# Attention's first score and query units: from two PSUM banks to six

## The chip, the cores and the metric

The kernel runs on one core of a Trainium2 chip, as one program. The metric is the device time in microseconds (us). The shown runs of the kernel before took 2261.34, 2261.57 and 2262.76 us; the median is 2261.57 us.

## The reference

The input `x` has 8 sequences of 2048 rows of 256 numbers, in fp32. The reference, cut to what matters:

```python
xn = layernorm(x)
qkv = xn @ W_qkv; q, k, v = split(qkv, 3)
scores = (q @ k.T) / sqrt(256), future positions masked
attn = softmax(scores) @ v                       # causal, one head, per sequence
ids = argmax(xn @ gate_w); s = sigmoid(max(xn @ gate_w))
shared = silu(xn @ sg) * (xn @ su) @ sd
routed = expert ids of (xn * s): silu(. @ rg) * (. @ ru) @ rd    # 32 experts, top 1
out = x + attn + shared + routed
```

## The kernel before

The program has three stages on all engines, one behind the other: tokens (layer norm, shared expert, values), experts (routed expert tiles), attention. Every fp32 product is made of three matmuls of rounded parts, high by high, low by high and high by low (`split_matmuls`, lines 87 to 89), so each operand is split into a high part (a copy on ScalarE, ACT in the profile) and a low part (a subtraction on VectorE, DVE, or on GpSimd, POOL).

Attention works on 32 groups of 512 query rows (4 in each sequence), and on tiles of a group by 128 keys. Tile t is (sequence, group in it, key block); there are 320. The first groups have 4, 8, 12 and 16 tiles: tiles 0 to 3 are group 0, 4 to 11 group 1, 12 to 23 group 2, and group 3 begins with tile 24. The last four tiles of a group lie on the diagonal: they are 512, 384, 256 and 128 columns wide. The queries are `x` times a product of the weights, so a score is a query unit times the normalized input.

**Units.** What TensorE (PE) writes for a score tile or for one half of a group's queries is a unit, and takes one PSUM bank. A full unit is six matmuls of 512 columns. Units are numbered in the order in which PE makes them: tiles 0 to 8 are units 0 to 8, then come query half (2, 0) as unit 9, tiles 9 and 10, query half (2, 1) as unit 12, tile 11 as unit 13, tiles 12 to 20 as units 14 to 22, and query half (3, 0) as unit 23. Here (g, c) is half c of group g. Tiles 0 and 1 are computed at the end of the expert stage (`first_scores`).

**Steps.** `Plan` writes out the order. The engines walk the same steps, each in its own queue. At a step, PE makes the query halves and the score tile of that step, broadcasts a group's maxima (line 1735), transposes a group's running maxima (`turn`, line 1728), and, from step 25 on (LAG), weighs the values with tile step - 25 (`weigh`, lines 1749 to 1753). ACT copies a unit out of PSUM (line 1672, or line 1663 for the high part of a query half) and takes the exponentials (lines 1679 and 1680). DVE takes the low part of a query half (line 1578), masks the diagonal (line 1592), keeps the running maximum (lines 1595 to 1613), reduces the transposed maxima (lines 1617 and 1621) and adds them to the scores (`lower`, line 1628). The four tiles of group 0 are lowered early, at steps 7 to 10, and exponentiated at steps 8 to 11; all others wait for their turn after step 23. The transposes of group 0 stand at step 5 and those of group 1 at step 13; the broadcasts stand two steps later. Score tile 12 is the first that needs the low part of query half (2, 1).

**Banks.** PSUM has 8 banks here: two for units (`psS`), two for maxima (`psX`), four for the weighted sums (`psO`). The four of `psO` are used by the expert stage under other names (`e_psT`, `e_psH`, two `e_psG`); in attention they lie unused until `weigh` of tile 0 at step 25. Unit n goes to bank n modulo 2, and `free_bank(n)` makes PE wait until unit n - 2 has been read: for a query half by DVE's subtraction, for a score tile by ACT's copy, DVE's mask and DVE's maximum.

**The other queues at this place.** SyncE (SP) ends the expert stage, then issues two loads of rows and ten loads of values (512 KB each), after GpSimd has set three small constants (lines 1556 to 1558), which the first broadcast waits for too. GpSimd then gathers routed rows, subtracts the low parts of the probabilities (line 1551) and adds up rows.

Of the kernel before, what the change touches and what calls it, by code (L numbers as in the profile page):

```python
# [19 lines left out]
F32 = mybir.dt.float32  # L20
# [1319 lines left out]
class Plan:  # L1340
# [3 lines left out]
    BANKS = 2  # L1344
# [3 lines left out]
    def __init__(self, B, NB, GB):  # L1348
        J = NB // GB
        self.J, self.GB = J, GB  # L1350
        self.tiles = [(b, G, j) for b in range(B) for G in range(GB) for j in range(J * (G + 1))]
        self.at = {tile: t for t, tile in enumerate(self.tiles)}
        self.T = len(self.tiles)
        self.first = [self.at[b, G, 0] for b in range(B) for G in range(GB)]
        self.last = [self.at[b, G, J * (G + 1) - 1] for b in range(B) for G in range(GB)]
        self.NGR = B * GB
        q_step = {}
        for g in range(2, self.NGR):
            for u in range(2):
                q_step.setdefault(max(0, self.first[g] - 3 + 2 * u), []).append((g, u))  # L1360
        self.q_step = q_step
        self.q_unit, self.s_unit = {}, []
        self.split, self.tops, self.reads, self.diags, self.acts = [], [], [], [], []
        self.turn_step = {}
        for g in range(self.NGR):
            self.turn_step.setdefault(self.first[g] + self.LAG - 8 if g >= 2 else self.last[g] + 2, []).append(g)
        self.lead = self.LAG - J - 8
        self.base_step = {}
        per = J * (GB + 1) * GB // 2
        for r in range(B * NB):  # L1370
            i = r % NB
            t = max(0, (r // NB) * per + (i * per // NB if r // NB < B - 1 else 7 * i // 4) - 8)
            self.base_step.setdefault(t + self.LAG - self.LOW, []).append(r)
        n = 0
        for t in range(self.T):
            for g, c in q_step.get(t, ()):
                self.q_unit[g, c] = n
                self.split.append(n)
                self.acts.append((self.acts[-1] if n else 0) + 1)
                n += 1  # L1380
            self.s_unit.append(n)
            _, G, j = self.tiles[t]
            diagonal, rest = self.diagonal(t), self.cut(t) < J - 1
            tops = self.tops[-1] if t else 0
            self.reads.append(tops + (rest if diagonal else j > 0))
            self.tops.append(self.reads[t] + diagonal)
            self.diags.append((self.diags[-1] if t else 0) + diagonal)
            self.acts.append((self.acts[-1] if n else 0) + (rest or not diagonal))
            n += 1
        self.splits = {n: k + 1 for k, n in enumerate(self.split)}  # L1390

    def tile_at(self, step, ahead):

# [33 lines left out]
def attention_stage(nc, ctx, block, sh_g, d_rows, xth_g, xtl_g, vh_g, vl_g, out_g, keep, ahead, D, B, N, ET):  # L1427
    C, NB, GB = D // P, N // P, N // GT
    J = GT // P
# [4 lines left out]
    SR = LAG - 1  # L1434
    NGR, R = plan.NGR, B * NB
    with ExitStack() as st:
# [3 lines left out]
        def ps(name, shape):  # L1440
            return st.enter_context(nc.psum_tensor("t_" + name, shape, F32))
# [23 lines left out]
        psS, psX = ahead.psS, ahead.psX  # L1465
        assert BANKS == psS.shape[1]
        psO = ps("psO", [P, J, 512])
        x_in = ahead.x_in
        v_in = [sem(f"v_in{k}") for k in range(VR)]
        r_in = [sem(f"r_in{k}") for k in range(2)]  # L1470
# [101 lines left out]
        def _(dve):  # L1572
            v = nc.vector

            def q_low(g, c):
                n = plan.q_unit[g, c]
                wait(dve, u_act, plan.acts[n])
                v.tensor_tensor(q_lo[:, g % QR, c], psS[:, n % BANKS], q_hi[:, g % QR, c].bitcast(F32),  # L1578
                                ALU.subtract).then_inc(split_ok, 1)

            def highest(t):
                n, g, c0 = plan.s_unit[t], plan.group(t), plan.cut(t) * P
                _, G, j = plan.tiles[t]
                m, s = top[:, g % TR], psS[:, n % BANKS]
                if j == 0 and G > 0:
                    return
                if plan.diagonal(t):
                    own, c1 = slice(c0, c0 + P), c0 + P
                    wait(dve, u_mm, n + 1)
                    wait(dve, u_act, plan.acts[n])  # L1590
                    wait(dve, lo_ok, t - SR + 1)
                    v.tensor_tensor(score[:, t % SR, own], s[:, own], keep.mask[:], ALU.add).then_inc(diag_ok, 1)
                    if j == 0:
                        wait(dve, top_mm, g - TR + 1)
                        v.tensor_copy(m[:, c1:], s[:, c1:]).then_inc(top_ok, 1)
                    else:
                        wait(dve, top_ok, plan.tops[t - 1])
                        if c1 < GT:
                            v.tensor_tensor(m[:, c1:], m[:, c1:], s[:, c1:], ALU.max).then_inc(top_ok, 1)
                    wait(dve, diag_ok, plan.diags[t])  # L1600
                    if j == 0:
                        v.tensor_copy(m[:, own], score[:, t % SR, own]).then_inc(top_ok, 1)
                    else:
                        v.tensor_tensor(m[:, own], m[:, own], score[:, t % SR, own], ALU.max).then_inc(top_ok, 1)
                    return
                wait(dve, u_act, plan.acts[n])
                if j < 2:
                    wait(dve, top_mm, g - TR + 1)
                if j == 1:
                    v.tensor_tensor(m[:], score[:, (t - 1) % SR], s[:], ALU.max).then_inc(top_ok, 1)  # L1610
                else:
                    wait(dve, top_ok, plan.tops[t - 1])
                    v.tensor_tensor(m[:], m[:], s[:], ALU.max).then_inc(top_ok, 1)  # L1613
# [40 lines left out]
        @block.scalar  # L1654
        def _(act):
            s = nc.scalar

            def q_high(g, c):
                n = plan.q_unit[g, c]
                wait(act, u_mm, n + 1)  # L1660
                if g >= QR:
                    wait(act, u_mm, plan.s_unit[plan.last[g - QR]] + 1)
                s.copy(q_hi[:, g % QR, c], psS[:, n % BANKS]).then_inc(u_act, 1)

            def keep_score(t):
                n = plan.s_unit[t]
                c0 = (plan.cut(t) + plan.diagonal(t)) * P
                if c0 == GT:
                    return
                wait(act, lo_ok, t - SR + 1)  # L1670
                wait(act, u_mm, n + 1)
                s.copy(score[:, t % SR, c0:], psS[:, n % BANKS, c0:]).then_inc(u_act, 1)  # L1672

            def exps(t):
                c0 = plan.cut(t) * P
                p = score[:, t % SR, c0:]
                wait(act, sub_ok, t + 1)
                wait(act, pv_mm, t - HR + 1)
                s.activation(p_hi[:, t % HR, c0:], p, ACT.Exp)  # L1679
                s.activation(p, p, ACT.Exp).then_inc(exp_ok, 1)  # L1680

            for step in range(T + LAG + 2):
                for g, c in plan.q_step.get(step, ()):
                    q_high(g, c)
                if step < T:
                    keep_score(step)
                t = plan.tile_at(step, plan.EXP)
                if t is not None:
                    exps(t)

        @block.tensor
        def _(pe):
            def free_bank(n):
                m = n - BANKS
                if m in plan.splits:
                    wait(pe, split_ok, plan.splits[m])
                elif m >= 0:
                    t = plan.s_unit.index(m)
                    wait(pe, u_act, plan.acts[m])
                    wait(pe, diag_ok, plan.diags[t])  # L1700
                    wait(pe, top_ok, plan.reads[t])

            def queries(g, c):
                n, k = plan.q_unit[g, c], g % XR
                if c == 0:
                    wait(pe, x_in[k], 32 * ((g + XR - GB) // XR))
                free_bank(n)
                project(nc, psS[:, n % BANKS], keep, x_hi[:, k], x_lo[:, k], c).then_inc(u_mm, 1)

            def scores(t):  # L1710
                n, g, c0 = plan.s_unit[t], plan.group(t), plan.cut(t) * P
# [4 lines left out]
                    wait(pe, split_ok, plan.splits[plan.q_unit[g, C - 1]])  # L1716
                free_bank(n)
                for d in range(C):
                    mm = split_matmuls(nc, psS[:, n % BANKS, c0:], x_hi[:, k, d, cols], x_lo[:, k, d, cols],
                                       q_hi[:, q, d, c0:], q_lo[:, q, d, c0:], d == 0, d == C - 1)  # L1720
                mm.then_inc(u_mm, 1)

# [15 lines left out]
            def weigh(t):  # L1738
# [5 lines left out]
                for a in range(plan.cut(t), J):  # L1744
                    cols = slice(a * P, (a + 1) * P)
                    last = j == J * G + a
                    if j == 0:
                        wait(pe, o_ok, (g - 1) * J + a + 1)
                    nc.tensor.matmul(psO[:, a, 0:W], p_hi[:, kp, cols], v_hi[:, kv, j % J], start=j == 0, stop=False,  # L1749
# [126 lines left out]
```

## Time and profile before

| what | value |
|---|---|
| median of the runs shown | 2261.57 us |
| time of the profiled execution | 2262.84 us |
| its span, first to last instruction | 2260.9 us |
| mean granted clock of TensorE | 0.998 |
| PE busy | 2228.1 us (99%) |
| DVE, ACT, POOL busy | 1637.5, 1159.9, 1073.5 us |

The span is what the profile's clock runs over: a position in the profile is us from its start. 1.94 us of the profiled execution lie outside. Attention's part begins near 1354.7 us. A matmul's row gives its start and its duration; matmuls are pipelined, so that the spacing of starts and not the duration says how fast they go. Idle time stands in brackets behind a row, with the instruction that ended it. [...]

### The profile page before, as it was taken

To read this page: it belongs to the slowest core of one execution; us is meant where nothing else is said; L and a number is where in the kernel's file an instruction comes from. 1 tells how busy PE (TensorE), PEld (TensorE's weight loads), DVE (VectorE), ACT (ScalarE), POOL (GpSimd) and SP (SyncE) were. 2 spreads that over 40 slices of the span, in tenths; PEclk is the share of its full clock that TensorE was granted. 3 is DMA by queue.
4 is the path that set the end of the run, shared out by engine and by line. 5 is a ranking of instruction groups with operands and counts; after the bars stand their busy time and mean duration, and the time that the engine had idled before them with its cause. 6 is when DMAs were issued, how large, how long until landed. Compare 5 with 4: busy or idle time off the path is not lost.

```text
span 2260.9 us, 46624 instructions
## 1 busy us (share of the span) xinstructions
PE 2228.1 (99%) x15254; PEld 2056.2 (91%) x15254; DVE 1637.5 (72%) x3543; ACT 1159.9 (51%) x2190; POOL 1073.5 (47%) x1016
## 2 busy tenths in 40 slices
PE   8999999999999999999999998999999999999998
PEld 7888888888888999999999997999999999999998
DVE  7777777777768987877878775666666667676755
ACT  4334334334344665665656654555555555555555
POOL 3333333333324434434434433666666666666677
PEclk9999999999999999999999999999999999999999
DMA  7665665665546877777787784243434343434341
GB/s 249 217 212 187 217 212 194 210 214 197 186 147 219 278 256 256 240 266 255 248 259 256 251 250 146 94 134 113 157 111 164 111 152 120 149 126 145 121 123 45
DMA packets 299531, 423.16 MB, mean 187 GB/s; under 512 B 35777, under 2 KB 216002, under 8 KB 299330
## 3 DMA queue, kind: packets, MB, share of 16 engines
q1 hardware_dynamic: 281986, 384.48, 50.6%
q0 software_dynamic: 17344, 36.27, 6.1%
q8 instruction: 93, 1.52, 0.3%
q14 instruction: 108, 0.88, 0.1%
HBM read 281.92 MB, written 138.74 MB: 186 GB/s over the span
## 4 chain that ended last, share of the span: by engine, by line
PE 94%; DVE 2%; POOL 1%; issue 1%; DMA 1%; ACT 1%; SPq 0%; POOLq 0%; ACTq 0%; DVEq 0%
PE ahead_psS L87 10%; PE ahead_psS L88 10%; PE ahead_psS L89 10%; PE ahead_psX L87 7%; PE ahead_psX L89 7%; PE ahead_psX L88 7%; PE t_psO L1749 6%; PE t_psO L1751 5%; PE t_psO L1753 5%; PE e_psG L87 3%; PE e_psG L89 3%; PE e_psG L88 3%; PE a_psD L89 3%; PE a_psD L87 3%; PE a_psD L88 3%; PE a_psT L87 1%
## 5 line engine op out<-in xcount | busy, mean ns | idle before, releaser
L1551 POOL TENSOR_TENSOR t_p_lo<-t_score,t_p_hi 128x512 fp32r<-128x512 f32 (+1 forms) x320 | 360.0, 1131 | 200.2 <-ACT t_score L1680 116.1
L1672 ACT COPY t_score<-ahead_psS 128x512 f32<-128x512 f32 (+3 forms) x288 | 148.4, 516 | 334.0 <-PE ahead_psS L89 288.7
L1749 PE MATMUL t_psO<-t_v_hi,t_p_hi 128*128 128x258 f32 x1088 | 313.4, 288 | 3.8 <-DVE ahead_dout L1637 2.5
L1751 PE MATMUL t_psO<-t_v_hi,t_p_lo 128*128 128x258 f32 x1088 | 307.6, 283 | 0.0
L1753 PE MATMUL t_psO<-t_v_lo,t_p_hi 128*128 128x256 f32 x1088 | 306.6, 282 | 0.0
L1067 POOL DMA_INDIRECT ahead_rows<-xs_rows,ahead_slot x144 | 175.8, 1221 | 206.3 <-PE e_psT L1247 162.3
L354 POOL DMA_INDIRECT token_of<-a_token_i,a_slot_i x128 | 140.6, 1099 | 244.5 <-DVE a_slot_i L465 206.8
L87 PE MATMUL ahead_psS<-ahead_q_hi,ahead_x_hi 128*128 128x512 f32 (+3 forms) x640 | 234.7, 367 | 7.2 <-DVE ahead_q_lo L1578 3.3
L88 PE MATMUL ahead_psS<-ahead_q_hi,ahead_x_lo 128*128 128x512 f32 (+3 forms) x640 | 233.9, 365 | 0.0
L89 PE MATMUL ahead_psS<-ahead_q_lo,ahead_x_hi 128*128 128x512 f32 (+3 forms) x640 | 233.2, 364 | 0.0
L1749 PEld LDWEIGHTS t_psO<-t_v_hi,t_p_hi 128*128 128x128 f32 x1088 | 206.0, 189 | 13.0 <-DVE ahead_dout L1637 3.0
L1751 PEld LDWEIGHTS t_psO<-t_v_hi,t_p_lo 128*128 128x128 f32 x1088 | 206.3, 190 | 8.2
L1753 PEld LDWEIGHTS t_psO<-t_v_lo,t_p_hi 128*128 128x128 f32 x1088 | 206.4, 190 | 0.0
L1613 DVE TENSOR_TENSOR t_top<-t_top,ahead_psS 128x512 f32<-128x512 f32 x144 | 98.9, 687 | 135.3 <-ACT t_score L1672 134.7
L1628 DVE TENSOR_TENSOR t_score<-ahead_psX,t_score 128x512 f32<-128x512 f32 (+1 forms) x320 | 190.2, 602 | 1.3 <-PE ahead_psX L1735 1.3
L1679 ACT ACTIVATE t_p_hi<-t_score 128x512 fp32r<-128x512 f32 (+1 forms) x320 | 182.6, 571 | 13.4 <-PE t_psO L1753 10.4
L1680 ACT ACTIVATE t_score<-t_score 128x512 f32<-128x512 f32 (+1 forms) x320 | 178.3, 557 | 0.0
L1535 POOL DMA_INDIRECT ahead_dout<-routed_rows,keep_position x128 | 123.0, 961 | 111.3 <-POOL ahead_raw L1543 59.3
L87 PE MATMUL ahead_psX<-e_whi,e_h_hi 128*128 128x256 f32 x576 | 161.9, 281 | 0.2 <-DVE e_h_lo L1109 0.2
L707 ACT ACTIVATE a_silu<-ahead_psX 128x512 f32<-128x512 f32 x128 | 76.5, 597 | 166.1 <-PE ahead_psX L89 161.3
L88 PE MATMUL ahead_psX<-e_whi,e_h_lo 128*128 128x256 f32 x576 | 161.6, 281 | 0.0
L89 PE MATMUL ahead_psX<-e_wlo,e_h_hi 128*128 128x256 f32 x576 | 161.6, 281 | 0.0
(266 smaller groups left out, 7180.5 us busy)
## 6 DMA issues: line engine op xcount, KB each, us to landing
ahead_raw<-in_L_ffn_routed_gate_w SPq DMA_DIRECT2D x42, 512.0 KB
ahead_raw<-in_L_ffn_routed_up_w SPq DMA_DIRECT2D x42, 512.0 KB
ahead_raw<-in_L_ffn_routed_down_w SPq DMA_DIRECT2D x41, 512.0 KB
e_raw<-in_L_ffn_routed_gate_w SPq DMA_DIRECT2D x41, 512.0 KB
e_raw<-in_L_ffn_routed_up_w SPq DMA_DIRECT2D x41, 512.0 KB
e_raw<-in_L_ffn_routed_down_w SPq DMA_DIRECT2D x41, 512.0 KB
a_xt<-in_L_attn_x SPq DMA_DIRECT2D x32, 512.0 KB, 6.0
v_high<-a_v_hi SPq DMA_DIRECT2D x32, 512.0 KB, 3.9
```

The lines of the kernel that those rows point to most:

```text
L87: nc.tensor.matmul(out, hi, rhi, start=first, stop=False, skip_group_check=True)
L88: nc.tensor.matmul(out, lo, rhi, start=False, stop=False, skip_group_check=True)
L89: return nc.tensor.matmul(out, hi, rlo, start=False, stop=last, skip_group_check=True)
L1067: g.indirect_dma_start(out=xg[:, k, h], out_offset=None, in_=xs, in_offset=bass.IndirectOffsetOnAxis(slot[:, s, h:h + 1], 0)).then_inc(x_i ...
L1551: g_.tensor_tensor(p_lo[:, t % LR, c0:], score[:, t % SR, c0:], p_hi[:, t % HR, c0:].bitcast(F32), ALU.subtract).then_inc(lo_ok, 1)
L1628: v.tensor_tensor(s, psX[:, g % 2, c0:], s, ALU.add).then_inc(sub_ok, 1)
L1672: s.copy(score[:, t % SR, c0:], psS[:, n % BANKS, c0:]).then_inc(u_act, 1)
L1679: s.activation(p_hi[:, t % HR, c0:], p, ACT.Exp)
L1680: s.activation(p, p, ACT.Exp).then_inc(exp_ok, 1)
L1749: nc.tensor.matmul(psO[:, a, 0:W], p_hi[:, kp, cols], v_hi[:, kv, j % J], start=j == 0, stop=False, skip_group_check=True)
L1751: nc.tensor.matmul(psO[:, a, 0:W], p_lo[:, t % LR, cols], v_hi[:, kv, j % J], start=False, stop=False, skip_group_check=True)
L1753: mm = nc.tensor.matmul(psO[:, a, 0:D], p_hi[:, kp, cols], v_lo[:, kv, j % J, 0:D], start=False, stop=last, skip_group_check=True)
```

## The change

`Plan` gives every unit a bank and remembers which unit had that bank before it. Units 0 and 1 keep banks 0 and 1. The units up to 20, which are those made before tile 19, go round six banks: 2, 3, 4, 5, 0, 1, and again; banks 2 to 5 are the four of `psO`. From unit 21 (tile 19) on it is bank n modulo 2 as before. `free_bank(n)` waits for the reads of the unit that had the bank before, and not at all where there was none. `weigh` of tile 0 waits, before its first matmul into each bank of `psO`, for the reads of the last unit there (units 20, 15, 16 and 17). All readers take the unit's bank from the same list. Nothing is computed otherwise, and no engine's order changes.

```diff
+        wide = self.s_unit[self.LAG - 6]
+        self.bank, self.former, latest = [], [], {}
+        for m in range(n):
+            if m < self.BANKS:
+                bank = m
+            elif m < wide:
+                bank = (m - self.BANKS) % (self.BANKS + J)
+                bank = bank + self.BANKS if bank < J else bank - J
+            else:
+                bank = m % self.BANKS
+            self.bank.append(bank)
+            self.former.append(latest.get(bank, -1))
+            latest[bank] = m
+        self.latest = {b: max(m for m in range(wide) if self.bank[m] == b) for b in range(self.BANKS, self.BANKS + J)}
...
+        unit = [psS[:, k] if k < BANKS else psO[:, k - BANKS] for k in plan.bank]
...
-            def free_bank(n):
-                m = n - BANKS
+            def read_out(m):
                 if m in plan.splits:
                     wait(pe, split_ok, plan.splits[m])
                 elif m >= 0:
...
+            def free_bank(n):
+                read_out(plan.former[n])
+
...
                     last = j == J * G + a
+                    if t == 0:
+                        read_out(plan.latest[BANKS + a])
                     if j == 0:
                         wait(pe, o_ok, (g - 1) * J + a + 1)
```

In `q_low`, `highest`, `q_high`, `keep_score`, `queries` and `scores`, `psS[:, n % BANKS]` becomes `unit[n]`.

## Rows read from the trace of the kernel before

**Rows 1.** The page: busy time of PE, and the chain by engine.
```profile
PE 2228.1 (99%) x15254; PEld 2056.2 (91%) x15254; DVE 1637.5 (72%) x3543; ACT 1159.9 (51%) x2190; POOL 1073.5 (47%) x1016
...
PE 94%; DVE 2%; POOL 1%; issue 1%; DMA 1%; ACT 1%; SPq 0%; POOLq 0%; ACTq 0%; DVEq 0%
```

**Rows 2.** Waits of PE, whole span: total us, times, longest.
```profile
PE ahead_psS L87 <- DVE ahead_q_lo L1578: 3.3, 4, 1.4
...
PE ahead_psS L87 <- DVE t_top L1602: 1.9, 1, 1.9
PE ahead_psS L87 <- DVE t_top L1610: 1.6, 2, 0.8
...
PE ahead_psS L87 <- DVE t_top L1599: 0.4, 1, 0.4
```

**Rows 3.** Waits of PE from 1402 us to the end.
```profile
PE t_psO L1749 <- DVE ahead_dout L1637: 2.5, 2, 2.3
PE t_psO L1749 <- POOL t_p_lo L1551: 1.2, 1, 1.2
```

**Rows 4.** Windows: busy us of PE, PEld, DVE, ACT, POOL; clock, DMA share, GB/s.
```profile
1358.00:1360.00 2.00, 1.58 (x7) 1.24 (x7) 1.18 (x5) 0.00 (x0) 0.00 (x0) 0.77 0.02 4
1360.00:1362.00 2.00, 2.00 (x7) 1.52 (x6) 0.00 (x0) 0.58 (x1) 0.32 (x3) 0.50 0.19 66
1362.00:1364.00 2.00, 2.00 (x11) 1.68 (x10) 0.23 (x1) 0.59 (x1) 0.97 (x1) 0.88 0.62 176
...
1372.00:1378.00 6.00, 3.79 (x20) 3.05 (x21) 4.87 (x12) 3.62 (x11) 3.93 (x5) 1.00 1.09 352
```

**Rows 5.** Timeline of PE: start, duration, line, operation, idle before and releaser.
```profile
1354.58 0.28 PE L89 MATMUL ahead_psX<-e_wlo,e_h_hi 128*128 128x256 f32 x1
...
1375.82 0.29 PE L87 MATMUL ahead_psS<-ahead_q_hi,ahead_x_hi 128*128 128x128 f32 x1
...
1376.39 0.28 PE L89 MATMUL ahead_psS<-ahead_q_lo,ahead_x_hi 128*128 128x128 f32 x1
...
1377.47 0.47 PE L87 MATMUL ahead_psS<-ahead_q_hi,ahead_x_hi 128*128 128x512 f32 x1 [0.81 <-DVE ahead_q_lo L1578]
...
1380.33 0.60 PE L1728 MATMUL ahead_psX<-keep_ident,t_top 128*128 128x128 f32 x4
1380.68 0.48 PE L87 MATMUL ahead_psS<-ahead_q_hi,ahead_x_hi 128*128 128x512 f32 x1
...
1389.37 0.47 PE L87 MATMUL ahead_psS<-ahead_q_hi,ahead_x_hi 128*128 128x512 f32 x1
...
1392.48 0.47 PE L87 MATMUL ahead_psS<-ahead_x_hi,keep_a_hi 128*128 128x512 f32 x1
...
1402.62 0.28 PE L1749 MATMUL t_psO<-t_v_hi,t_p_hi 128*128 128x258 f32 x1
```

**Rows 6.** Timeline of DVE, 1363 to 1376 us.
```profile
1363.77 0.69 DVE L1617 TENSOR_REDUCE t_negmax<-ahead_psX 128x4 f32<-128x512 f32 x1 [4.38 <-PE ahead_psX L1728]
...
1372.66 0.69 DVE L1578 TENSOR_TENSOR ahead_q_lo<-ahead_psS,ahead_q_hi 128x512 fp32r<-128x512 f32 x1 [1.91 <-ACT ahead_q_hi L1663]
1373.27 0.41 DVE L1628 TENSOR_TENSOR t_score<-ahead_psX,t_score 128x256 f32<-128x256 f32 x1
...
1374.12 0.85 DVE L1604 TENSOR_TENSOR t_top<-t_top,t_score 128x128 f32<-128x128 f32 x1
...
1375.58 0.69 DVE L1604 TENSOR_TENSOR t_top<-t_top,t_score 128x128 f32<-128x128 f32 x1
```

**Rows 7.** Timeline of ACT: copy of tile 8 and what follows it.
```profile
1369.21 0.48 ACT L1672 COPY t_score<-ahead_psS 128x384 f32<-128x384 f32 x1 [1.03 <-PE ahead_psS L89]
1369.71 1.28 ACT L1679 ACT_TABLE_LOAD   x1
```

**Rows 8.** Timeline of POOL: last of three constants; last gather before weighing.
```profile
1361.46 0.13 POOL L1558 MEMSET t_v_hi<- 128x20 f32 x1
...
1389.30 0.96 POOL L1535 DMA_INDIRECT ahead_dout<-routed_rows,keep_position  x1 [0.83 <-POOL ahead_raw L1543]
```

More of the change, by code:

```diff
@@ L1577, in q_low @@
                 wait(dve, u_act, plan.acts[n])
-                v.tensor_tensor(q_lo[:, g % QR, c], psS[:, n % BANKS], q_hi[:, g % QR, c].bitcast(F32),
+                v.tensor_tensor(q_lo[:, g % QR, c], unit[n], q_hi[:, g % QR, c].bitcast(F32),
                                 ALU.subtract).then_inc(split_ok, 1)
@@ L1583, in highest @@
                 _, G, j = plan.tiles[t]
-                m, s = top[:, g % TR], psS[:, n % BANKS]
+                m, s = top[:, g % TR], unit[n]
                 if j == 0 and G > 0:
@@ L1662, in q_high @@
                     wait(act, u_mm, plan.s_unit[plan.last[g - QR]] + 1)
-                s.copy(q_hi[:, g % QR, c], psS[:, n % BANKS]).then_inc(u_act, 1)
+                s.copy(q_hi[:, g % QR, c], unit[n]).then_inc(u_act, 1)
             def keep_score(t):
@@ L1671, in keep_score @@
                 wait(act, u_mm, n + 1)
-                s.copy(score[:, t % SR, c0:], psS[:, n % BANKS, c0:]).then_inc(u_act, 1)
+                s.copy(score[:, t % SR, c0:], unit[n][:, c0:]).then_inc(u_act, 1)
             def exps(t):
@@ L1707, in queries @@
                 free_bank(n)
-                project(nc, psS[:, n % BANKS], keep, x_hi[:, k], x_lo[:, k], c).then_inc(u_mm, 1)
+                project(nc, unit[n], keep, x_hi[:, k], x_lo[:, k], c).then_inc(u_mm, 1)
             def scores(t):
@@ L1718, in scores @@
                 for d in range(C):
-                    mm = split_matmuls(nc, psS[:, n % BANKS, c0:], x_hi[:, k, d, cols], x_lo[:, k, d, cols],
+                    mm = split_matmuls(nc, unit[n][:, c0:], x_hi[:, k, d, cols], x_lo[:, k, d, cols],
                                        q_hi[:, q, d, c0:], q_lo[:, q, d, c0:], d == 0, d == C - 1)
```

## The prediction

> **What bounds the kernel now.** I read the page first. PE is busy 2228.1 of 2260.9 us and holds 94% of the chain that ended last [rows 1]: a microsecond that PE saves is kept, unless another engine then becomes late. Next come the waits of PE over the whole span. Waits of score and query units for DVE's reads amount to 3.3 + 1.9 + 1.6 + 0.4 = 7.2 us [rows 2], all of them between 1356 and 1400 us, where attention begins. The reader is to see there that the releasers are the last readers of a unit two places earlier: with two banks, PE makes a unit and the one after it, and then stands until DVE has done with the first. After 1402 us PE waits 3.7 us in three places, all near the end, for DVE's outputs and POOL's low parts [rows 3]; no bank wait is left there, since weighing a tile lies between two units. So the question is how far PE's clock of events moves up between 1354.7 us, where the last expert matmul ends its turn [rows 5], and 1392.48 us, where query half (3, 0) begins [rows 5]. From there both kernels have two banks and the same order.
>
> The listed waits are not the whole loss. In the windows of 2 us from 1358 to 1364 us the granted clock reads 0.77, 0.50 and 0.88 [rows 4]: time lost is 2 x 0.23 + 2 x 0.50 + 2 x 0.12 = 1.7 us. It follows the longest bank wait, 1.9 us [rows 2]. And tiles 19 and 20 with their banks take 1392.48 - 1389.37 = 3.11 us [rows 5], where two units at full pace take 1380.33 - 1377.47 = 2.86 us: two banks cost 0.25 us per pair of full units even where hardly any wait is listed, because copy and maximum come one behind the other before the bank is free.
>
> **The change part by part.** It adds no engine instruction; it changes which waits stand ahead of a unit. I walk PE's order from 1354.70 us (1354.58 plus 0.12 for the last expert matmul's turn). Prices: a full unit 2.86 / 2 = 1.43 us; a 128-column unit 1376.39 + 0.11 - 1375.82 = 0.68 us; the transposes of a group 1380.68 - 1380.33 = 0.35 us [rows 5]; 384 and 256 columns by width, estimates of 1.07 and 0.72 us; a broadcast, one matmul of 512 columns, a sixth of a unit, 0.24 us.
>
> *Step 2 to step 11.* Tiles 2 to 5 go to banks that attention has not used, and the bank of each later unit was read long before. Tile 2 ends at 1355.42, tile 3 at 1356.10, tiles 4 and 5 at 1358.96. The transposes of group 0 need DVE's maxima of tile 3. DVE's work on tiles 0 to 3 is now free of the waits for PE within it, and I take it to be just in time; where it isn't, the price is that of the shortest listed wait for such a maximum, 0.4 us [rows 2]. After transposes and tiles 6 and 7 PE is at 1362.17 and broadcasts. DVE's reduction and spread, two operations of 0.69 us [rows 6] started near 1359.6, are done at 1361.0; the constants are done at 1361.46 + 0.13 = 1361.6 [rows 8], and no part of the change moves them. That margin is 0.6 us and would be the next thing late. Tile 8 then ends at 1362.17 + 0.24 + 1.43 = 1363.84. PE goes on with query half (2, 0), tiles 9 and 10, query half (2, 1) and tile 11: 1.43 + 1.07 + 0.72 + 1.43 + 0.68 = 5.33, so 1369.2 us.
>
> *Step 12.* Tile 12 needs the low part of (2, 1), a data wait that no bank takes away. Before it was the 0.81 us at 1377.47 [rows 5]; now it grows, since PE arrives earlier than the two engines that split the queries. ACT begins the copy of tile 8 about 0.2 us behind PE, at 1364.05, where it began at 1369.21 [rows 7]. Behind it stand the table load of 1.28 us, the exponentials of tile 0, and the high part of (2, 0). The distance from that copy to DVE's low part was 1372.66 - 1369.21 = 3.45 us [rows 6, 7] with no other wait in it, so DVE starts at 1367.50. From there DVE is the limit: low part 0.61, then lowering and masking for tiles 2, 9, 3 and 10, which took from 1373.27 to 1375.58 + 0.61 = 1376.19, or 2.92 us without idle time [rows 6]. The low part of (2, 1) runs from 1371.03 to 1371.72, and tile 12 starts at 1371.8. ACT's high part of (2, 1) doesn't decide: it comes behind that of (2, 0) with six short copies and exponentials of at most some 0.5 us between, 3.5 us in all from 1366.9, so by 1370.5 at the latest, an estimate. PE's wait is 2.6 us. Two of DVE's maxima in this stretch took 0.85 and 0.69 us where others of that form take 0.28, both while POOL subtracts [rows 6]; if they miss POOL now, tile 12 comes 1.0 us earlier. I keep them, since POOL's subtractions hang on the same exponentials.
>
> *Step 12 to query half (3, 0).* Tiles 12 and 13 take 2.86, the transposes of group 1 0.35: 1375.0. Tiles 14 to 18 have free banks: 5 x 1.43 + 0.24 = 7.39, so PE is ready for tile 19 at 1382.4. Tile 19 is the first with two banks again and needs that of tile 17, begun at 1375.0 + 3 x 1.43 + 0.24 = 1379.53; at the pace of a pair, 3.11, it begins at 1382.6. Half (3, 0) comes 3.11 later, at 1385.8 us. It was at 1392.48: **6.7 us earlier**. In parts: bank waits and slower pace taken away, 1.7 us of clock given back, less the longer wait for query half (2, 1).
>
> *What follows.* Weighing starts at step 25, 1402.62 before [rows 5], 1395.9 now. The low parts of tiles 0 to 3, the values and the first gathered rows are all there even unmoved: POOL's last gather before weighing ends at 1390.3 us [rows 8], so nothing there is met too early. The four added waits of the first weighing are for units 20 and 15 to 17, read some 10 us earlier: nothing, or at most 0.4 us for PE's queue to take them, what the shortest listed wait costs [rows 2]. All else is behind PE: SP's loads, stores and POOL's rows wait on PE's or DVE's progress and move up with it. The waits near the end [rows 3] stay as they are.
>
> The profiled execution took 2262.84 us for its span of 2260.9; with 6.7 us off, its span would be 2254.2 and its time 2256.1. It lies 1.3 us above the median shown, so the median goes from 2261.57 to **2254.9 us**.
>
> **A rule on the clock.** The trace shows 0.50 behind a wait of 1.9 us, but 1.00 from 1372 to 1378 us with idle times of 1.4 and 0.8 us in it [rows 2, 4, 5]. [...]
>
> **The rivals.**
>
> *The clock falls behind the new gap.* The 2.6 us wait ahead of tile 12 is longer than the 1.9 us wait that a fall followed, and a narrow unit stands before it, as there. Against it: PE works without a break for 14 us before, which it did not then. The price is that of the old fall, 1.7 us: 2256.6 us. Decided by the clock between 1369 and 1378 us.
>
> *The advance is given back.* Something that does not move with PE holds the first weighings or the end: POOL's row gathers and SP's loads from 1362 us on, or POOL, which already releases PE near the end [rows 3]. For it: DMA's share reads 1.09 from 1372 to 1378 us [rows 4]. Against it: 5.6 us between POOL's last gather [rows 8] and 1395.9. If two thirds of the gain went, 2259.3 us. The change failing to do what it says, because ACT and DVE and not banks set the pace, gives the same: if DVE's part from tile 8 to (2, 1) came only 2 us sooner, 2259.6.
>
> *Slower: the clock stays low.* If the fall behind the new gap didn't end in some 3.5 us but held, each us at 0.50 would cost half a us. [...] For it only that the gap is the longest in attention; against it, the fall of before ended while bank waits went on, and PE has 50 us without one behind 1403 us.
>
> **How the numbers follow.** What a measurement of this kernel can tell from no change is 0.2%, 4.5 us: faster means under 2257.05. Chances: my forecast 0.58, the clock behind the new gap 0.26, the advance given back 0.12, slower 0.04. The first two are faster: 0.84. Given back is within 0.2%: 0.12. The forecast's own spread is 1.0 us faster for DVE's two maxima, 0.04 us for each of 15 full units if they run at 1.39, together 1.6, and 0.6 slower for queues and fresh starts: 2253.3 to 2255.5. With the fall, up to 2257.2. I set the range from 2252.8 to 2258.0; what is left out is most of the last two cases.
>
> **What would show it.** In the new profile: no bank wait of PE from 1354 to 1369 us; the clock 1.00 from 1356 to 1366; broadcast of group 0 at 1362.2; tile 12 at 1371.8, behind a wait of 2.6 us for DVE's low part; (3, 0) at 1385.8 and weighing from 1395.9; the wait total for units down from 7.2 to about 4; rows near the end as before, 6.7 us earlier. It would be wrong if a transfer or the constants released PE at the first broadcast, if tile 12 stayed beyond 1374, or if the waits near the end grew.

## The result and the profile after

The changed kernel takes 2254.41 us (median of 11 runs, 2252.43 to 2257.61) and the kernel before 2261.06 us (11 runs, 2258.11 to 2263.90): ratio 0.9972, 95% interval 0.9963 to 0.9980. That is 6.3 us less, between 4.5 and 8.4; the difference of the medians is 6.65 us. The forecast was 6.7 and 2254.9 us. The profiled execution took 2256.52 us for a span of 2254.6, 6.3 us less than the span before.

The page of the changed kernel, answering to [rows 1]. The bound is the same: of the 6.3 us of span, 1.5 us are less busy time of PE and 4.8 us less idle time.

```profile
PE 2226.6 (99%) x15254; PEld 2057.8 (91%) x15254; DVE 1637.5 (73%) x3543; ACT 1160.0 (51%) x2190; POOL 1075.2 (48%) x1016
```

Waits of PE in the changed kernel over the whole span, answering to [rows 2, 3]. Columns: total us, times, longest.

```profile
PE t_psO L87 <- DVE ahead_q_lo L1593: 2.1, 1, 2.1
...
PE t_psO L1768 <- DVE ahead_dout L1652: 1.7, 2, 1.1
...
PE ahead_psS L87 <- DVE ahead_q_lo L1593: 1.3, 2, 0.9
PE t_psO L1768 <- POOL t_p_lo L1566: 1.2, 1, 1.2
PE ahead_psX L1752 <- POOL t_v_hi L1573: 0.7, 1, 0.7
```

The reader is to see that every wait of a unit for DVE's maxima (`t_top`) is gone; those were 1.9 + 1.6 + 0.4 us. What is left is one long wait for the low part of query half (2, 1), two small ones near half (3, 1) (its own low part, and the bank of half (3, 0)), and a new one of 0.7 us at the first broadcast, for the constants.

Timeline of PE in the changed kernel, answering to [rows 5]: transposes of group 0, first broadcast, tile 12, transposes of group 1, tile 14, tile 19, half (3, 0), first weighing.

```profile
1358.64 0.60 PE L1745 MATMUL ahead_psX<-keep_ident,t_top 128*128 128x128 f32 x4
...
1362.67 0.50 PE L1752 MATMUL ahead_psX<-t_spread,t_ones 128*128 128x512 f32 x1 [0.67 <-POOL t_v_hi L1573]
...
1371.80 0.50 PE L87 MATMUL t_psO<-ahead_q_hi,ahead_x_hi 128*128 128x512 f32 x1 [2.08 <-DVE ahead_q_lo L1593]
...
1376.24 0.60 PE L1745 MATMUL ahead_psX<-keep_ident,t_top 128*128 128x128 f32 x4
1376.59 0.48 PE L87 MATMUL t_psO<-ahead_q_hi,ahead_x_hi 128*128 128x512 f32 x1
...
1384.06 0.47 PE L87 MATMUL ahead_psS<-ahead_q_hi,ahead_x_hi 128*128 128x512 f32 x1
...
1387.17 0.47 PE L87 MATMUL ahead_psS<-ahead_x_hi,keep_a_hi 128*128 128x512 f32 x1
...
1397.08 0.28 PE L1768 MATMUL t_psO<-t_v_hi,t_p_hi 128*128 128x258 f32 x1
```

Windows of the changed kernel, answering to [rows 4]; the granted clock, as a share of full speed, is the third number from the end.

```profile
1358.00:1360.00 2.00, 2.00 (x12) 1.63 (x11) 1.07 (x3) 0.65 (x2) 0.00 (x0) 1.00 0.03 7
...
1370.00:1372.00 2.00, 0.20 (x1) 0.20 (x2) 1.94 (x7) 0.88 (x3) 1.77 (x4) 1.00 1.07 355
1372.00:1374.00 2.00, 2.00 (x6) 1.57 (x6) 0.43 (x1) 0.00 (x0) 1.17 (x2) 0.55 1.09 353
1374.00:1376.00 2.00, 2.00 (x6) 1.54 (x6) 0.00 (x0) 0.58 (x1) 1.14 (x3) 0.60 1.09 352
1376.00:1378.00 2.00, 2.00 (x12) 1.68 (x11) 1.09 (x2) 0.59 (x1) 0.67 (x1) 1.00 1.11 357
```

The fall of the clock near 1359 us [rows 4] is gone, and a fall of the same price, 2 x 0.45 + 2 x 0.40 = 1.7 us, stands behind PE's gap ahead of tile 12. Tiles 12 and 13 therefore take 1376.24 - 1371.80 = 4.44 us where they took 2.86. This was the first rival.

DVE, ACT and POOL in the changed kernel, answering to [rows 6, 7, 8]: low part of (2, 0), the next operation, the two maxima, low part of (2, 1); copy of tile 8 and table load; the first and the last of the constants.

```profile
1368.04 0.69 DVE L1593 TENSOR_TENSOR ahead_q_lo<-t_psO,ahead_q_hi 128x512 fp32r<-128x512 f32 x1 [1.91 <-ACT ahead_q_hi L1678]
1368.65 0.41 DVE L1643 TENSOR_TENSOR t_score<-ahead_psX,t_score 128x256 f32<-128x256 f32 x1
...
1369.51 0.84 DVE L1619 TENSOR_TENSOR t_top<-t_top,t_score 128x128 f32<-128x128 f32 x1
...
1370.86 0.28 DVE L1619 TENSOR_TENSOR t_top<-t_top,t_score 128x128 f32<-128x128 f32 x1
1371.06 0.68 DVE L1593 TENSOR_TENSOR ahead_q_lo<-ahead_psS,ahead_q_hi 128x512 fp32r<-128x512 f32 x1
```

```profile
1364.60 0.48 ACT L1687 COPY t_score<-t_psO 128x384 f32<-128x384 f32 x1 [1.97 <-PE t_psO L89]
1365.09 1.28 ACT L1694 ACT_TABLE_LOAD   x1
```

```profile
1362.30 0.20 POOL L1571 MEMSET t_ones<- 128x128 f32 x1 [17.20 <-SPq L1056]
...
1362.48 0.13 POOL L1573 MEMSET t_v_hi<- 128x20 f32 x1
```

From the last expert tile's second half of work (PE's row with the wait for `e_h_lo`, 1353.17 before, 1353.00 after) to the first weighing is the stretch that the change works on; I call it the stretch. It took 1402.62 - 1353.17 = 49.45 us and now 1397.08 - 1353.00 = 44.08. So of the 6.3 us of span, 0.17 lie ahead of it, 5.37 in it, and 0.76 behind it, where the waits near the end read 2.9 us instead of 3.7.

### The profile page after: what moved, and what is told of

Same layout as the page of the kernel before. It is cut to its first block, busy times and chain, and to the rows that moved or that the text cites. A ratio compares the mean times of both kernels' runs of the same rounds, so it can differ in the third digit from the quotient of the medians.

```text
span 2254.6 us, 46624 instructions
## 1 busy us (share of the span) xinstructions
PE 2226.6 (99%) x15254; PEld 2057.8 (91%) x15254; DVE 1637.5 (73%) x3543; ACT 1160.0 (51%) x2190; POOL 1075.2 (48%) x1016
## 4 chain that ended last, share of the span: by engine, by line
PE 94%; DVE 2%; issue 1%; POOL 1%; DMA 1%; ACT 1%; SPq 0%; POOLq 0%; DVEq 0%; ACTq 0%
PE ahead_psS L87 10%; PE ahead_psS L88 10%; PE ahead_psS L89 10%; PE ahead_psX L87 7%; PE ahead_psX L89 7%; PE ahead_psX L88 7%; PE t_psO L1768 6%; PE t_psO L1770 5%; PE t_psO L1772 5%; PE e_psG L87 3%; PE e_psG L88 3%; PE e_psG L89 3%; PE a_psD L89 3%; PE a_psD L87 3%; PE a_psD L88 3%; PE a_psT L87 1%
## 5 line engine op out<-in xcount | busy, mean ns | idle before, releaser
L1687 ACT COPY t_score<-ahead_psS 128x512 f32<-128x512 f32 (+3 forms) x277 | 142.9, 516 | 317.5 <-PE ahead_psS L89 276.3
L87 PE MATMUL ahead_psS<-ahead_q_hi,ahead_x_hi 128*128 128x512 f32 (+2 forms) x616 | 224.7, 365 | 1.4 <-DVE ahead_q_lo L1593 1.3
L88 PE MATMUL ahead_psS<-ahead_q_hi,ahead_x_lo 128*128 128x512 f32 (+2 forms) x616 | 224.8, 365 | 0.0
L89 PE MATMUL ahead_psS<-ahead_q_lo,ahead_x_hi 128*128 128x512 f32 (+2 forms) x616 | 224.0, 364 | 0.0
```

What stands on the lines that cost most here:

```text
L87: nc.tensor.matmul(out, hi, rhi, start=first, stop=False, skip_group_check=True)
L88: nc.tensor.matmul(out, lo, rhi, start=False, stop=False, skip_group_check=True)
L89: return nc.tensor.matmul(out, hi, rlo, start=False, stop=last, skip_group_check=True)
L1687: s.copy(score[:, t % SR, c0:], unit[n][:, c0:]).then_inc(u_act, 1)
```

## The experiments

All are compared with the kernel before on the same chip. Single executions of one kernel spread over 4 to 6 us, so that the timing alone tells few of these edits apart; the stretch of the profiled execution does, once it is seen whether the clock fell in it. The stretch comes from one profile of each edit, so a difference of some 0.5 us, which is what the two profiles of the changed kernel differ by, says little. A second profile of the changed kernel is among the runs.

**The old waits on six banks** (`e1_old_waits`).

```diff
             def free_bank(n):
+                read_out(n - BANKS)
                 read_out(plan.former[n])
```

> The changed kernel with its six banks, but each unit also waits for the reads of unit n - 2, as with two banks. Theory A (the waits for the reads were the cost, the banks themselves are free): the bank waits ahead of tile 2 (1.9 us), tile 4, tile 7 and of tile 10 come back, the clock falls near 1359 us and not behind tile 11, and the time is that of the kernel before, ratio 1.000 within 0.001. Theory B (ACT and DVE set the pace, the gain comes from which banks are read and written side by side): the gain of some 6.5 us stays, ratio near 0.997.

Measured: ratio 1.0003 (0.9994 to 1.0012), median 2262.64 us. The whole gain is gone, with the banks of the changed kernel. Its timeline of PE shows the old wait ahead of tile 2, now for a bank that nobody uses, and the first weighing. The waits ahead of tiles 4, 7 and 10 are back too (0.42, 0.87 and 1.32 us). Its windows show no fall of the clock:

```profile
1356.69 0.36 PE L87 MATMUL t_psO<-ahead_q_hi,ahead_x_hi 128*128 128x256 f32 x1 [1.89 <-DVE t_top L1617]
...
1401.79 0.28 PE L1769 MATMUL t_psO<-t_v_hi,t_p_hi 128*128 128x258 f32 x1
```

```profile
1358.00:1360.00 2.00, 1.58 (x9) 1.25 (x9) 1.18 (x5) 0.00 (x0) 0.00 (x0) 1.00 0.02 7
1360.00:1362.00 2.00, 2.00 (x13) 1.68 (x12) 0.00 (x0) 0.88 (x2) 0.07 (x1) 1.00 0.19 66
```

Theory A holds for the waits, and is wrong on one point: the same wait of 1.89 us, behind which the clock read 0.50 in [rows 4], left it at 1.00 here. The stretch, 1401.79 - 1353.12 = 48.67 us, is 0.9 us more than the old 49.45 less a fall of 1.7. Up to tile 12 it is the old one: tile 12 starts 22.79 us after the stretch begins, and 24.30 before, fall of 1.7 included. From tile 12 to the first weighing it takes 25.88 us for 25.15. There two units have 0.19 us of idle time that waits for nothing the profile shows; that the doubled waits ahead of each unit cause this is likely, and no run here tests it.

**Six banks only before tile 12** (`e2_wide12`).

```diff
-        wide = self.s_unit[self.LAG - 6]
+        wide = self.s_unit[12]
```

> Six banks only for units before tile 12; from tile 12 on two banks. Theory A: tile 12 starts at 1371.8 us as in the changed kernel, and the stretch from tile 14 to query half (3, 0), 10.6 us with six banks and 11.8 with two, takes 11.8 us again: 1.2 us slower than the changed kernel, so some 5.3 us faster than the kernel before, ratio 0.9977. Theory B (what six banks do after tile 12 is lost anyway in the wait for query half (3, 1), where PE meets ACT and DVE again): same as the changed kernel, ratio 0.9971.

Measured: ratio 0.9971 (0.9959 to 0.9982), median 2254.65 us. That is theory B's ratio, but by timing a kernel 1.2 us slower can't be told from the changed one. The profile tells more: tile 12 stands where forecast, behind a gap as long as there, and yet the clock does not fall.

```profile
1371.63 0.47 PE L87 MATMUL ahead_psS<-ahead_q_hi,ahead_x_hi 128*128 128x512 f32 x1 [2.15 <-DVE ahead_q_lo L1593]
...
1374.80 0.48 PE L87 MATMUL ahead_psS<-ahead_q_hi,ahead_x_hi 128*128 128x512 f32 x1
...
1377.25 0.47 PE L87 MATMUL ahead_psS<-ahead_q_hi,ahead_x_hi 128*128 128x512 f32 x1 [0.81 <-DVE t_top L1625]
...
1386.57 0.48 PE L87 MATMUL ahead_psS<-ahead_x_hi,keep_a_hi 128*128 128x512 f32 x1
...
1396.76 0.28 PE L1768 MATMUL t_psO<-t_v_hi,t_p_hi 128*128 128x258 f32 x1
```

```profile
1372.00:1374.00 2.00, 2.00 (x11) 1.65 (x10) 0.22 (x1) 0.59 (x1) 1.14 (x3) 1.00 1.09 355
```

From tile 14 (1374.80) to half (3, 0) (1386.57) PE takes 11.77 us, as in the kernel before (11.80), where the changed kernel takes 10.58; theory A had 11.8. From there to the first weighing it takes 10.19 us, for 9.91 in the changed kernel. Together the second half of the six banks is worth 1.5 us, and the first half the rest. The clock read 1.00 in all of these parts, so no fall has to be taken off. Theory B falls in this profile: what PE wins after tile 12 is not eaten by the wait for (3, 1). The whole stretch is 1396.76 - 1353.10 = 43.66 us without a fall; the changed kernel without one would be at 44.08 - 1.7 = 42.4, or at 41.8 by its second profile below.

**Filling the gap** (`e3_filler`).

```diff
+                if t == plan.first[2]:
+                    free_bank(n)
+                    project(nc, unit[n], keep, x_hi[:, 2], x_lo[:, 2], 0)
                 if g >= 2:
                     wait(pe, split_ok, plan.splits[plan.q_unit[g, C - 1]])
```

> The changed kernel plus six matmuls of 512 columns, 1.4 us, written into the bank of tile 12 ahead of its data wait; the tile then overwrites them, so the output is unchanged. They fill most of PE's gap of 2.5 us. Theory A (the idle gap makes the clock fall to 0.50 behind it, at a price of 1.7 us): granted clock 1.00 from 1370 to 1378 us, tile 12 still at 1371.8, tiles 12 and 13 take 2.9 us and not 4.4, weighing begins 1.6 us sooner, about 1395.5, ratio near 0.9965. Rival (the clock falls from something else than idle time, such as DMA traffic at a share of 1.09, or needs no gap): the fall stays, ratio as for the changed kernel, 0.9972.

Measured: ratio 0.9967 (0.9955 to 0.9979), median 2254.23 us. The gap is 0.67 us, the clock 1.00, with DMA's share at 1.09 as ever:

```profile
1371.93 0.50 PE L87 MATMUL t_psO<-ahead_q_hi,ahead_x_hi 128*128 128x512 f32 x1 [0.67 <-DVE ahead_q_lo L1593]
```

```profile
1372.00:1374.00 2.00, 2.00 (x9) 1.66 (x10) 0.50 (x2) 0.38 (x1) 1.16 (x2) 1.00 1.09 356
```

The stretch is 1395.62 - 1354.06 = 41.56 us, 2.5 less than the changed kernel's. The clock's fall didn't follow the traffic: with the same DMA share of 1.09 it reads 1.00 here and in the kernel before [rows 4], and there it fell where the share was 0.02. That filling the gap is what kept it up is one profile's word, since the run before also kept it, with the gap in place; the table below adds to it.

**The table load early** (`e4_early_table`): one exponential of 128 x 1 on ACT at step 4.

```diff
+                if step == 4:
+                    s.activation(warm[:], keep.ident[:, 0:1], ACT.Exp)
                 if step < T:
                     keep_score(step)
```

> The changed kernel plus one exponential of 128 x 1 on ACT at step 4, where ACT is idle for 1.5 us, so that the table load of 1.28 us stands there and not between the copy of tile 8 and the split of query half (2, 0). Theory A (the chain from tile 8 over ACT and DVE to query half (2, 1) sets tile 12): no table load near 1365 us, tile 12 at 1370.5, PE's gap down from 2.5 to 1.2 us, and if so short a gap leaves the clock at 1.00, 1.3 + 1.7 = 3.0 us gained on the changed kernel, ratio near 0.996; with the fall left in place 1.3 us, ratio 0.9966. Rival (PE's own broadcast, or DVE's maxima behind POOL, sets tile 12): no change from the changed kernel.

Measured: ratio 0.9966 (0.9952 to 0.9979), median 2254.64 us. ACT's timeline has the load between the copies of tiles 2 and 4, and PE's gap ahead of tile 12 is 0.79 us with the clock at 1.00:

```profile
1357.51 1.28 ACT L1702 ACT_TABLE_LOAD   x1
1358.81 0.20 ACT L1702 ACTIVATE t_warm<-keep_ident 128x1 f32<-128x1 f32 x1
...
1365.13 0.48 ACT L1688 COPY t_score<-t_psO 128x384 f32<-128x384 f32 x1 [1.04 <-PE t_psO L89]
```

```profile
1367.17 0.69 DVE L1594 TENSOR_TENSOR ahead_q_lo<-t_psO,ahead_q_hi 128x512 fp32r<-128x512 f32 x1 [0.50 <-ACT ahead_q_hi L1679]
```

```profile
1371.05 0.53 PE L87 MATMUL t_psO<-ahead_q_hi,ahead_x_hi 128*128 128x512 f32 x1 [0.79 <-DVE ahead_q_lo L1594]
```

From the copy of tile 8 to the low part of (2, 0) it is now 1367.17 - 1365.13 = 2.04 us, where it was 3.44 (1368.04 - 1364.60): 1.4 us out of the chain. The stretch is 1394.84 - 1354.48 = 40.36 us: 1.5 us below the 41.8 of an undisturbed changed kernel, theory A's 1.3. The profiled time, 2256.65 us, doesn't show it: the stretch began 1.5 us later than in the changed kernel's first profile (1354.48 for 1353.00), and near 2230 us PE waited 2.55 us for an output, behind which the clock's fall cost 3.4 us, where there it cost 1.7.

**The changed kernel again** (`after_again`), unedited.

> The changed kernel once more, for a second profile. Theory A, as mended after the first four runs (a gap of 2 us makes the clock fall in some executions and not in others): stretch from the last expert matmuls (row with the wait for e_h_lo) to the first weighing 44.1 us with the fall and 42.4 us without, and the kernel's own mean time about 0.8 us above its undisturbed 2254. Rival (the fall belongs to this kernel): the fall is there again, 44.1 us. The constants come when the last expert transfers allow, so PE's wait for them at the first broadcast may be between 0 and 1 us.

Measured: ratio 0.9971 (0.9962 to 0.9981), median 2254.59 us, as the first time. The stretch is 1395.72 - 1352.18 = 43.54 us, with a fall behind the same gap, and no wait at the first broadcast:

```profile
1372.00:1374.00 2.00, 2.00 (x6) 1.59 (x5) 0.00 (x0) 0.59 (x1) 1.42 (x2) 0.50 1.09 358
```

Without the fall it would be 41.8 us. The two profiles differ by 0.54 us, about the 0.67 us wait for the constants.

**Six banks up to tile 24** (`e5_wide24`): `wide = self.s_unit[self.LAG - 1]`.

> Six banks for all units before tile 24 and not only before tile 19. Theory A: the bank waits ahead of tile 19, query half (3, 0) and tile 22 go, half (3, 1) begins 1.5 us sooner after tile 18 than in the changed kernel, and tile 24 still waits for its low part, some 3.1 us behind the start of (3, 1): 1.4 us faster than the changed kernel, ratio 0.9966. Rival (the wait for (3, 1) is set by DVE, which is not sooner, and eats it): ratio as for the changed kernel, 0.9972.

Measured: ratio 0.9963 (0.9950 to 0.9977), median 2252.67 us; stretch 1392.78 - 1351.26 = 41.52 us with a fall of the clock, 2.0 us under the 43.54 of the changed kernel on the same chip, which has a fall too. Of this, 1.6 us lie behind tile 14, where the banks differ (18.98 us from there to the first weighing, for 20.55), and the rest ahead of it. Theory A, with a little more than the 1.4 forecast: PE's only wait between tile 12 and the first weighing is the 0.78 us for half (3, 1), in place of 0.42 and 0.87.

**Ones set early** (`e7_early_ones`): the matrix of ones in a place of its own, set before `raw_idle` is waited for; the first broadcast waits for it alone, the first weighing for all three constants.

```diff
+            g_.memset(ones[:].bitcast(F32), 1.0).then_inc(ones_ok, 1)
             pool.wait_ge(u_act, 1)
             pool.wait_ge(ahead.raw_idle, 1)
-            g_.memset(ones[:].bitcast(F32), 1.0).then_inc(ones_ok, 1)
...
                 if g == 0:
-                    pe.wait_ge(ones_ok, 3)
+                    pe.wait_ge(ones_ok, 1)
```

> The changed kernel with the matrix of ones in a place of its own, set before the expert stage's last transfers are waited for; the first broadcast waits for it alone. Theory A: PE's wait at the first broadcast, 0.67 us in the changed kernel's profile and 0.31 in that with two banks from tile 12, is gone; the whole chain behind it (lowering, table load, splits) moves up and tile 12 with it: 0.3 to 0.7 us faster than the changed kernel, too little for the timing to tell. Rival (table load or DVE have slack there): tile 12 stays and its wait grows by the same 0.3 to 0.7 us.

Measured: ratio 0.9977 (0.9967 to 0.9987), median 2255.89 us; stretch 1395.84 - 1352.66 = 43.18 us with a fall. No wait stands at the broadcast: it started at 1361.51 us, and the other two constants were done only at 1362.18. The stretch is 0.9 us shorter than in the changed kernel's first profile and 0.4 shorter than in its second, where the constants came in time. The median is 1.3 us above that of the changed kernel on the same chip, within the intervals; six of its nine runs read a mean clock of 0.997, against two of ten there. By timing it is inconclusive. By the rows the wait can't come any more, theory A; what it is worth is what the constants are late in an execution, 0 to 0.7 us here.

**All together** (`e8_all`): early table load, early ones, six banks up to tile 24.

> Early table load, early ones, and six banks up to tile 24, together. Theory A: the parts add up: 1.3 us of table load, up to 0.7 of constants, 1.4 of banks, and a gap ahead of tile 12 of about 1 us, behind which the clock no longer falls: 3.4 to 4.1 us faster than the changed kernel without a fall, up to 5.8 with one; stretch to the first weighing 39 us, ratio 0.9952. Rival (ACT or DVE becomes the limit of the whole stretch, so that the parts overlap): stretch not under 40.4 us, ratio 0.996.

Measured: ratio 0.9953 (0.9939 to 0.9967), median 2251.66 us: the best version by ratio, 2.9 us under the changed kernel on the same chip, with intervals that just touch (0.9967 and 0.9962). The stretch is 1393.23 - 1354.57 = 38.66 us without a fall, behind a gap of 0.79 us:

```profile
1371.13 0.50 PE L87 MATMUL t_psO<-ahead_q_hi,ahead_x_hi 128*128 128x512 f32 x1 [0.79 <-DVE ahead_q_lo L1594]
```

The parts add up, against the rival's 40.4 us or more.

**Four banks** (`e10_four_banks`): `bank = (m - self.BANKS) % 4`, so that two of the weighted sums' banks are used.

> The changed kernel with four banks in turn instead of six (two of the weighted sums' four). Theory A: what PE needs is to be let past DVE's chain for group 0 and the two splits; by the changed kernel's rows no unit up to tile 18 is read later than three full units behind its own end, so four banks give nearly all: at most one short bank wait, ratio within 0.0004 of the changed kernel's 0.9972. Rival (all six are needed because PE runs up to five units ahead before tile 6): a wait of 0.5 to 1.5 us ahead of tile 6 or 7, a third of the gain lost, ratio 0.998.

Measured: ratio 0.9974 (0.9965 to 0.9984), median 2254.30 us; stretch 1395.60 - 1351.71 = 43.89 us with a fall, 0.35 us more than the changed kernel's second profile. One wait of some size comes, ahead of tile 4, which was not where the rival put it:

```profile
1355.28 0.47 PE L87 MATMUL ahead_psS<-ahead_q_hi,ahead_x_hi 128*128 128x512 f32 x1 [0.55 <-DVE t_top L1617]
```

**The early table load with two banks** (`e6_before_table`): the edit of `e4_early_table` in the kernel before.

> The kernel before, with two banks, and the table load moved to ACT's step 4 as in the run with the changed kernel. Theory A (there too the chain over the table load releases PE, at the wait of 1.42 us ahead of tile 10): that wait goes, 1.3 us faster than the kernel before, ratio 0.9994. Rival (with two banks the bank waits take over what the table load gives): ratio 1.000, the wait ahead of tile 10 replaced by others.

Measured: ratio 0.9994 (0.9985 to 1.0003), median 2258.80 us; stretch 1401.66 - 1353.29 = 48.37 us with a fall, 1.1 less than before, which had a fall too. The wait ahead of tile 10 went from 1.42 to 0.30 us:

```profile
1372.41 0.39 PE L87 MATMUL ahead_psS<-ahead_q_hi,ahead_x_hi 128*128 128x256 f32 x1 [0.30 <-DVE ahead_q_lo L1579]
```

So the chain over the table load set PE's pace there even with two banks. The timing's interval includes no change at all; the stretch speaks for theory A.

**Queries earlier as well** (`e11_all_early_q`): as all together, with the halves of group 2 at steps 8 and 9.

> Early table load, early ones, six banks up to tile 24, and the halves of query group 2 made at steps 8 and 9 instead of 9 and 11, so that PE has tiles 9 to 11 between the second half and tile 12. Theory A: the data wait ahead of tile 12 (0.79 us) goes or stays under 0.3; stretch to the first weighing 38.0 us, ratio near 0.995. Rival (ACT and DVE take the splits before their other work and the exponentials and maxima move behind them, so that something else waits, as tile 12 or the transposes of group 1): stretch 38.7 us or more.

Measured: ratio 0.9957 (0.9944 to 0.9971), median 2251.92 us; stretch 1391.05 - 1353.41 = 37.64 us. PE no longer waits ahead of tile 12, theory A, and the stretch is 1.0 us shorter than with all together; by timing the two are alike.

The profiles side by side; "gap" is PE's longest listed wait in the stretch, and "fell" whether a window behind it reads under 0.9:

| kernel | stretch, us | gap, us | fell |
|---|---|---|---|
| before | 49.45 | 1.89 | yes |
| old waits | 48.67 | 1.89 | no |
| before, early table | 48.37 | 1.89 | yes |
| changed | 44.08 | 2.08 | yes |
| changed, again | 43.54 | 2.07 | yes |
| four banks | 43.89 | 2.06 | yes |
| ones early | 43.18 | 2.10 | yes |
| banks to tile 24 | 41.52 | 2.06 | yes |
| banks to tile 12 | 43.66 | 2.15 | no |
| filled gap | 41.56 | 0.88 | no |
| early table | 40.36 | 0.87 | no |
| all | 38.66 | 0.79 | no |
| all, early queries | 37.64 | 0.78 | no |

## Why the prediction was right, and where it was not

*What bounds the kernel.* Right. PE is the bound, the stretch is where the change works, and what is won there stays: behind the first weighing the rest took 858.3 us before and 857.5 after.

*The waits are the cost.* Right, and shown by the old waits on six banks: with the banks of the changed kernel the ratio is 1.0003. The bank waits listed for PE, and the slower pace of a pair with two banks, are both gone: tiles 14 to 18 with a broadcast took 8.7 us before, from 1380.68 to 1389.37 [rows 5], and from 1376.59 to 1384.06, 7.5 us, now. The run with two banks from tile 12 puts that second half at 1.5 us, where my walk had it at about 1.

*Step 2 to step 11.* Right on PE's own work: the transposes at 1358.64 (forecast 1358.96). The margin at the first broadcast, 0.6 us with the constants held to be fixed at 1361.6, was wrong: they came at 1362.6 and cost 0.67 us. Counted from the start of the stretch they were done after 8.4 us before, 9.6 in the changed kernel and 9.0 in its second profile, where PE needs them after 9.0. POOL sets them when SP's queue lets it go, behind the last expert transfers, and this point moved by 1.2 us from one execution to the next. I had named them as the next thing late, and should have priced them.

*Step 12.* Right to the hundredth, at 1371.80 us, but by two errors that cancel: DVE's chain began 0.54 us late, at 1368.04 for 1367.50, through the constants; and only one of the two maxima took long (0.84 and 0.28 us, for 0.85 and 0.69). The long one, at 1369.51 us, stands beside POOL's subtractions, which run from 1369.20 to 1370.94, and the short one, at 1370.86, hardly does; that POOL is the cause stays unproven, since three other operations of DVE on 128 columns beside it took their usual 0.27 to 0.28 us. The wait reads 2.08 us in the list and 1371.80 - 1369.55 = 2.25 from the last matmul's turn, where I had 2.6: PE was done with tile 11 at 1369.55 us, not 1369.2. That ACT's table load is in this chain is shown by moving it: 1.5 us off the stretch, and 1.1 even with two banks.

*The clock.* This is the term that failed. "1.7 us of clock given back" was in the sum; the fall moved behind the new gap instead, in both profiles of the changed kernel. I gave that 0.26. From tile 12 to tile 14 it took 4.79 us for 3.2, so tile 14 came at 1376.59, 1.6 us after the forecast, and half (3, 0) at 1387.17 for 1385.8. In the stretch a fall followed a gap of 1.9 to 2.15 us in seven of nine profiles, and came in none of the four whose longest gap was 0.9 us or less. So the fall is neither sure nor absent at such a gap, and one profile can't price it; that the changed kernel has it about as often as the kernel before is likely, but counted in too few profiles to be shown.

*The sum.* The time came out at 6.65 us all the same, and that is in good part luck. Against the 6.7 us of the forecast the two profiles read: 1.6 lost to the fall; 0.2 won from tile 14 to half (3, 0), 10.58 for 10.8 us, since full units take 1.37 to 1.39 us in an unbroken row and not 1.43; 0.2 won from there to the first weighing, 9.91 us for the old 10.14; and 0.8 won behind it, the waits near the end, which I had held fixed. That makes 6.3 us, the difference of the spans. The last term is not shown to be the change's: the same waits add up to 2.1 us in the second profile of the changed kernel and to 4.1 in the run with the early table load. Had both kernels been profiled without a fall in the stretch, the stretches would be 47.75 and 41.8 to 42.4 us, 5.4 to 5.9 us apart; that is my best reading of what the change itself is worth in the stretch, and the timing, 6.65 us with an interval from 4.5 to 8.4, doesn't speak against it.

*The clock with two banks.* In the kernel before, pairs of units with two banks read 1.00 from 1364 us to the first weighing, with idle times of up to 1.42 us between them, and in the stretch the fall came only behind gaps near 2 us, 1.89 to 2.10 us.

*The rivals.* The first, the clock behind the new gap, happened in its mechanism, at its price of 1.7 us; that the time stayed nearer to the forecast than to its 2256.6 is the luck told above. The advance was not given back: first weighing 5.5 us earlier, POOL's gathers done before. The clock didn't stay low: it was back at 1.00 by 1376 us.

## What to carry to other kernels

Banks that a later phase owns are free buffers for the phase before it, and a producer that is the bound should be let past its readers there; four banks gave nearly all of what six gave here, a stretch of 43.89 us for 43.54. When the waits for buffers go, look for the data wait that comes forward, here the split of the next queries, for which PE waited 0.81 us before and 2.08 us after, and shorten its chain. Moving the table load took 1.5 us off the stretch, and making the query halves earlier another 1.0; neither shows in the median by itself. The table load, the early ones and six banks up to tile 24 together stood 2.9 us lower in the median. Where single executions spread over 5 us, measure the stretch between two named instructions in the profile, and note whether the clock fell in it.

## What the runs showed of the hardware

The clock of PE fell from 1.00 to about 0.50 for some 3.4 us, a loss of 1.7 us, in some executions of a kernel and not in others, behind the same gap: 1.89 us with and without a fall, 2.06 to 2.15 us five times with and once without. Where PE waits 2.2 to 3.7 us near 709 us, in the expert stage, it fell in 11 of the 13 profiles, and not in two, whose gaps were 2.41 and 2.59 us:

```profile
708.98 0.38 PE L87 MATMUL e_psG<-e_x_hi,e_whi 128*128 128x256 f32 x1 [2.49 <-DVE e_x_lo L1098]
```

```profile
710.00:712.00 2.00, 2.00 (x12) 2.00 (x11) 2.00 (x4) 0.08 (x1) 0.00 (x0) 0.50 0.36 124
```

It also fell once behind shorter gaps that stand close together. Near the end of the changed kernel a fall of 1.7 us came behind waits of 1.10 and 0.57 us, and none behind the same two waits in the run with six banks only before tile 12:

```profile
2227.67 0.39 PE L1768 MATMUL t_psO<-t_v_hi,t_p_hi 128*128 128x258 f32 x1 [1.10 <-DVE ahead_dout L1652]
2228.86 0.53 PE L1768 MATMUL t_psO<-t_v_hi,t_p_hi 128*128 128x258 f32 x1 [0.57 <-DVE ahead_dout L1652]
```

Such falls are a part of the spread of single executions. Of the 11 runs of the changed kernel the four with a mean clock of 0.999 or more took 2253.3 us in the mean, and the seven others 2255.8.
